# A bf16 copy for the transposes of quantised activations, in a fused two-layer AdaLN/FFN kernel

## What is computed

```python
def _fake_quant_lastdim(x):
    s = jnp.max(jnp.abs(x), axis=-1, keepdims=True) / QMAX      # QMAX = 127
    s = jnp.maximum(s, 1e-08)
    return jnp.clip(jnp.round(x / s), -QMAX, QMAX) * s

def _dyn_quant_linear(x, w, b):
    return jnp.einsum('bti,oi->bto', _fake_quant_lastdim(x), _fake_quant_lastdim(w)) + b

h = jnp.einsum('bij,bkj->bik', x, weight[adapter_ids])          # "l0"
h = _layernorm(h, gamma, beta)
h = _dyn_quant_linear(h, w1, b1)
h = jax.nn.gelu(h, approximate=False)
h = _dyn_quant_linear(h, w3, b3)
x = x + h
```

## Time and profile before

| | us |
|---|---|
| median of 3 runs | 876.65 |
| lowest, highest | 874.74, 877.16 |
| the profiled execution, its own time | 874.75 |
| its span, first to last instruction | 872.8 |

### The profile page before, as it was taken

The page is one execution under the profiler, slowest core; times in us unless marked ns, Lnnn a source line. Parts: engine busy times, 40 slices in busy tenths (PEclk is TensorE's granted clock), DMA queues, the critical chain, the costliest instruction groups (busy, mean ns, idle before and its releaser), DMA issues.

```text
span 872.8 us, 11055 instructions
## 1 busy us (share of the span) xinstructions
PE 761.2 (87%) x3172; PEld 488.5 (56%) x3172; DVE 578.2 (66%) x2036; ACT 335.4 (38%) x577; POOL 64.7 (7%) x34
## 2 busy tenths in 40 slices
PE   4989899989899999998968899999898892699656
PEld 2544444344444444444645788887687771587445
DVE  6555282434675656483746524438999998899998
ACT  0333733304534252434324633444333421757152
POOL 0002000202621011022020000000000000000000
PEclk9999999989999999999999899999999996899969
DMA  8994654133448353512031345334333249653103
GB/s 340 374 334 163 240 179 171 60 111 140 159 149 355 108 189 139 193 56 89 24 121 50 129 161 182 115 114 159 122 128 108 102 155 411 272 193 121 48 35 158
DMA packets 40297, 140.94 MB, mean 161 GB/s; under 512 B 8511, under 2 KB 9663, under 8 KB 34626
## 3 DMA queue, kind: packets, MB, share of 16 engines
q1 hardware_dynamic: 38962, 137.72, 43.8%
q10 hardware_dynamic: 1296, 2.74, 0.8%
HBM read 106.86 MB, written 33.58 MB: 161 GB/s over the span
## 4 chain that ended last, share of the span: by engine, by line
PE 49%; DVE 34%; ACT 8%; issue 5%; DMA 2%; POOL 1%; DVEq 0%; SPq 0%; ACTq 0%
PE PS L779 21%; PE PS L837 12%; PE PS L947 8%; DVE ksum L1361 6%; DVE kprod L1356 6%; DVE ka L1365 4%; DVE nr L1438 4%; DVE kb L1365 3%; PE PS L826 2%; ACT qT L542 2%; DVE xr L1283 2%; PE PS L868 2%; DMA x_raw<-x_tr_dram 2%; PE PS L794 1%; DVE xp L1268 1%
## 5 line engine op out<-in xcount | busy, mean ns | idle before, releaser
L779 PE MATMUL PS<-w_raw,x_raw 128*128 128x512 f32 x512 | 230.4, 604 | 13.7 <-DMA x_raw<-x_tr_dram 11.0
L779 PEld LDWEIGHTS PS<-w_raw,x_raw 128*128 128x128 f32 x512 | 96.7, 194 | 124.9 <-issue 124.1
L947 PE MATMUL PS<-w_hi,xT_hi 128*128 128x512 f32 x256 | 105.0, 410 | 0.0
L947 PE MATMUL PS<-w_lo,xT_hi 128*128 128x512 f32 x256 | 102.0, 399 | 0.0
L947 PE MATMUL PS<-w_hi,xT_lo 128*128 128x512 f32 x256 | 101.7, 397 | 0.0
L1361 DVE TENSOR_REDUCE ksum<-kprod 128x16 f32<-128x64 f32 x392 | 75.2, 233 | 0.2 <-issue 0.2
L837 PE MATMUL PS<-w3q,qT 128*128 128x512 bf16 x256 | 61.3, 395 | 14.4 <-ACT qT L542 14.4
L1131 DVE SCALAR_TENSOR_TENSOR gbuf<-PS,lnst,vecs 128x512 f32<-128x512 f32 x32 | 23.7, 749 | 75.0 <-PE PS L837 75.0
L542 ACT ACTIVATE qT<-PS,round_c 128x512 bf16<-128x512 f32 x64 | 40.3, 679 | 84.4 <-PE PS L826 84.3
L837 PE MATMUL PS<-w1q,qT 128*128 128x512 bf16 x256 | 60.4, 391 | 8.4 <-DVE x1buf L1149 5.7
L470 POOL TENSOR_TENSOR xres<-xres,vecs 128x1024 f32<-128x1024 f32 x16 | 42.2, 2659 | 329.8 <-DMA xres<-x_tok_dram 329.8
(11 more groups left out here) (165 smaller groups left out, 1128.2 us busy)
## 6 DMA issues: line engine op xcount, KB each, us to landing
w_raw<-cond_w_dram SPq DMA_DIRECT2D x32, 1024.0 KB, 5.6
stage<-w_dram SPq DMA_DIRECT2D x16, 512.0 KB, 12.1
x_raw<-x_tr_dram SPq DMA_DIRECT2D x32, 256.0 KB, 6.4
xres<-x_tok_dram SPq DMA_DIRECT2D x8, 1024.0 KB, 9.3
x_scratch<-x1buf SPq DMA_DIRECT2D x16, 512.0 KB, 6.4
x1n<-x_scratch SPq DMA_DIRECT2D x16, 512.0 KB, 5.7
xr<-x_scratch SPq DMA_DIRECT2D x16, 512.0 KB, 3.6
y_scratch<-y SPq DMA_DIRECT2D x16, 512.0 KB, 3.6
```

Of the source, the lines that this page charges most:

```text
L779: mm = pe.matmul(PS[:, 2 * t + h, :], x_raw[pr][:, c, t * P:(t + 1) * P], w_raw[pr][:, c, h * H2:(h + 1) * H2], start=(pr == 0 and c == 0) ...
L947: pe.matmul(PS[:, 2 * t + h, :], xx[:, c, t * P:(t + 1) * P], ws[c // 2][:, c % 2, h * H2:(h + 1) * H2], start=(c == 0 and xx is xT_hi and ...
```

## The change

ScalarE gets a second ACTIVATE behind each quantising one: it reads the f32 tile, subtracts `ROUND` and writes a bf16 copy `q16[t]`. It waits on a semaphore (`r1_done`, `r2_done`) for the first. The integers from -127 to 127 are exact in bf16. TensorE transposes `q16[t]` with a bf16 identity, all eight blocks into one bank (8 x 128 bf16 columns fill its 2 KB): tile 0 uses `T_BANK`, tile 1 `T_BANK + 1`. `evac_T` becomes one ACTIVATE of 128x1024, a plain copy, which waits for all eight. To make room, `av_hi` and `av_lo` shrink to the 56 columns in use (`AW`), and what reads them follows. VectorE makes the bf16 identity at the start.

```diff
+    AW = 32 + NH
...
+        ident16 = sb("ident16", [P, P], BF16)
+        av_hi = sb("av_hi", [P, KC, AW], F32R)
+        av_lo = sb("av_lo", [P, KC, AW], F32R)
...
+        q16 = [sa(f"q16{t}", [P, D], BF16) for t in range(NTOK)]
...
             def quant1(s, t):
                 act.wait_ge(ln_step, LN_OPS * (NTOK * s + t + 1))
                 nc.scalar.activation(hbuf[t][:, :], hbuf[t][:, :], ACT.Identity, bias=round_c[:, 0:1],
-                                     scale=lnst[:, t, 9:10]).then_inc(q1_done, 1)
+                                     scale=lnst[:, t, 9:10]).then_inc(r1_done, 1)
+                act.wait_ge(r1_done, NTOK * s + t + 1)
+                nc.scalar.activation(q16[t][:, :], hbuf[t][:, :], ACT.Identity, bias=round_c[:, 1:2]).then_inc(q1_done, 1)
...
             def evac_T(s, t, which):
...
-                for h in range(2):
-                    act.wait_ge(done, 4 * s + 2 * t + h + 1)
-                    nc.scalar.activation(qT[t][:, 4 * h:4 * h + 4, :],
-                                         PS[:, T_BANK + h, :].rearrange("p (c n) -> p c n", c=4),
-                                         ACT.Identity, bias=round_c[:, 1:2]).then_inc(ev, 1)
+                act.wait_ge(done, 4 * s + 2 * t + 2)
+                nc.scalar.activation(qT[t][:, :, :], PS[:, T_BANK + t, :].bitcast(BF16).rearrange("p (c n) -> p c n", c=KC),
+                                     ACT.Copy).then_inc(ev, 2)
...
             def transposes(s, t, which):
-                q, done, src = (q1_done, t1_done, hbuf) if which == 1 else (q2_done, t3_done, gbuf)
+                q, done = (q1_done, t1_done) if which == 1 else (q2_done, t3_done)
                 pe.wait_ge(q, NTOK * s + t + 1)
+                t_bank_free(s, t, which)
+                bank = PS[:, T_BANK + t, :].bitcast(BF16)
                 for h in range(2):
-                    t_bank_free(s, t, which, h)
-                    for c in range(4):
-                        tr = pe.transpose(PS[:, T_BANK + h, c * P:(c + 1) * P],
-                                          src[t][:, (4 * h + c) * P:(4 * h + c + 1) * P], ident[:, :])
+                    for c in range(4 * h, 4 * h + 4):
+                        tr = pe.transpose(bank[:, c * P:(c + 1) * P], q16[t][:, c * P:(c + 1) * P], ident16[:, :])
                     tr.then_inc(done, 1)
...
-                        mm = pe.matmul(PS[:, LL_BANK, 0:S], a[:, c, :], xx[:, c, :],
+                        mm = pe.matmul(PS[0:AW, LL_BANK, 0:S], a[:, c, :], xx[:, c, :],
...
+            dve.wait_ge(id_set, 1)
+            nc.vector.tensor_copy(ident16[:, :], ident[:, :]).then_inc(id16_set, 1)
```

More of the change, by code:

```diff
@@ L88, in adaln_ffn @@
         ident = sb("ident", [P, P], F32)
-        av_hi = sb("av_hi", [P, KC, P], F32R)
-        av_lo = sb("av_lo", [P, KC, P], F32R)
+        ident16 = sb("ident16", [P, P], BF16)
+        av_hi = sb("av_hi", [P, KC, AW], F32R)
+        av_lo = sb("av_lo", [P, KC, AW], F32R)
         zall = sb("zall", [P, NT, NH], F32)
@@ L162, in adaln_ffn @@
         vec_ld, bias_ld, ids_ld, ones_set = sem("vec_ld"), sem("bias_ld"), sem("ids_ld"), sem("ones_set")
-        id_zero, id_set = sem("id_zero"), sem("id_set")
+        id_zero, id_set, id16_set = sem("id_zero"), sem("id_set"), sem("id16_set")
+        r1_done, r2_done = sem("r1_done"), sem("r2_done")
         misc_ld, wb_split, b_set, b_ld = sem("misc_ld"), sem("wb_split"), sem("b_set"), sem("b_ld")
@@ L530, in quant2 @@
                 nc.scalar.activation(gbuf[t][:, :], gbuf[t][:, :], ACT.Identity, bias=round_c[:, 0:1],
-                                     scale=q2st[:, t, 2:3]).then_inc(q2_done, 1)
+                                     scale=q2st[:, t, 2:3]).then_inc(r2_done, 1)
+                act.wait_ge(r2_done, NTOK * s + t + 1)
+                nc.scalar.activation(q16[t][:, :], gbuf[t][:, :], ACT.Identity, bias=round_c[:, 1:2]).then_inc(q2_done, 1)
             def evac_T(s, t, which):
@@ L652, in evac_ll @@
                 act.wait_ge(ll_done, b + 1)
-                nc.scalar.activation(fbuf[:, :], PS[:, LL_BANK, 0:S], ACT.Copy)
+                nc.scalar.activation(fbuf[0:AW, :], PS[0:AW, LL_BANK, 0:S], ACT.Copy)
                 nc.scalar.activation(ls[0:RANK, :], PS[0:RANK, LL_BANK, 0:S], ACT.Copy)
@@ L769, in _ @@
             pe.wait_ge(id_set, 1)
+            pe.wait_ge(id16_set, 1)
             def l0(s, pr):
@@ L796, in stage_T, with t_bank_free @@
                     tr.then_inc(st_T, 1)
-            def t_bank_free(s, t, which, h):
+            def t_bank_free(s, t, which):
                 if which == 1 and s == 0:
-                    pe.wait_ge(st_ev, 2 * (KC + 3 + 2 * t) + h + 1)
-                elif which == 3 and s == 0 and t == 0:
-                    pe.wait_ge(st_ev, 2 * (KC + 7) + h + 1)
-                elif which == 3 and s == NB - 2 and t == 0:
-                    pe.wait_ge(xl_done, 2 + h + 1)
-                elif t == 1:
-                    pe.wait_ge(e1_done if which == 1 else e3_done, 4 * s + h + 1)
+                    pe.wait_ge(st_ev, 2 * (KC + 3 + 2 * t) + 2)
+                elif which == 3 and s == 0:
+                    pe.wait_ge(st_ev, 2 * (KC + 7) + 2)
+                elif which == 3 and s == NB - 2:
+                    pe.wait_ge(xl_done, 4)
                 elif which == 1:
-                    wait(pe, e3_done, 4 * (s - 1) + 2 + h + 1)
+                    pe.wait_ge(e3_done, 4 * (s - 1) + 2 * t + 2)
                 else:
-                    pe.wait_ge(e1_done, 4 * s + 2 + h + 1)
+                    pe.wait_ge(e1_done, 4 * s + 2 * t + 2)
             def o_bank_free(s, t, which, h):
@@ L960, in heads @@
                 for t in range(NTOK):
-                    pe.matmul(PS[:, LG_BANK, t * NH:(t + 1) * NH], fbuf[:, t * P:(t + 1) * P], ident[:, VC:VC + NH],
+                    pe.matmul(PS[:, LG_BANK, t * NH:(t + 1) * NH], fbuf[0:AW, t * P:(t + 1) * P], ident[0:AW, VC:VC + NH],
                               start=True, stop=False)
```

## The result

The changed kernel takes 889.09 us, median of 4 runs (887.36 to 889.62), against 875.69 for the kernel before (4 runs, 872.34 to 877.16): a ratio of 1.0155, 95% interval 1.0121 to 1.0189. It is slower by 13.4 us. The forecast was 7.5 us and 884.2, in a range of 876.5 to 890. So the direction, the mechanism and the range held, and the size was off by 5 to 6 us. The profiled execution has 889.62 us as its own time and a span of 887.5.

What follows compares the result with a forecast made beforehand. TensorE is nearly full, but ScalarE's queue ends each step on a TensorE stall. Path changes of +0.8 us plus clock falls of +6.7 make +7.5, added to the 876.65 median: 884.2, range 876.5 to 890.

Steps and rivals of the forecast that it cites:

- The walk: Running sum of delays from start to tail, clock aside: +0.8 us at the end of the span.
- the start's 0.74 + 1.16: Start: first transposes wait for both evacuations, +0.74; a copy delays later evacuations, 1.16; given as +1.8 at `l0(2,0)`.
- rival 3: Transposes don't get shorter, the weight load setting the pace: +10.3 us, 887; chance 0.07.
- the stall chain: `quant2`, copy and evacuation ahead of `product(s-1,0,3)` at a step's end: net +0.91 us where on the path.
- the places at the edge: `product(s-1,0,3)` in steps 4, 5, 6 and `product(6,0,3)`: idles of 2.36 or some 2.3 us; half counted, 3.4.
- the larger ones: Start's last weight block, `l0(4,3)`, `product(7,0,3)`: idles of 2.99, 2.7, 3.1 us; three quarters counted, 3.3.
- the seven: All places where a lengthened stall might drop TensorE's clock, four at the edge and three larger: 11.1 us if all fall.
- its own sign: Forecast wrong if a step's chain no longer passes through the copy, or idles of 2.4 leave the clock at 1.00.
- the av weights: 24 narrower matmuls in `low_and_heads` of 0 and 1: 0.25 us off twice, bounds 0 and -0.6.
- the clock holds: Rival: clock stays up in all or all but one place, 877.5 to 879.1; chance 0.15.
- the kernel is faster: Rival: copy cheap or hidden in ScalarE's queue between `quant2` and `evac_T`; -2.6, or -9.6 if off the path; chance 0.08.
- It falls everywhere: Rival: the clock falls at every listed place, 888.6 us; chance 0.10.

Runs made afterwards that it cites:

- experiment 12: Kernel before, with tile 0's second evacuation ahead of tile 1's gelu (steps 3 to 6) and step 4's x_raw requested right behind the base weights; 868.02 us.
- experiment 4: Kernel before with only the av weights narrowed from 128 to 56 columns; 877.04 us, ratio 1.0017.
- Experiment 3: Changed kernel with eight extra bf16 matmuls filling TensorE's stall in each of steps 4 to 7; 887.78 us, ratio 1.0131.
- experiment 1: Kernel before plus the copies, which nobody reads, and the narrow av weights; transposes stay f32; 890.2 us, ratio 1.0183.
- experiment 5: Changed kernel with the heads' products contracting over all 128 rows again; 887.52 us, ratio 1.0145.
- experiments 2 and 7: Changed kernel without copies: in 2 quantising writes bf16 without rounding, 873.43 us; in 7 it writes fp16 with 1536 added, 873.52 us.
- experiment 6: Changed kernel with all 32 copies, some moved back in ScalarE's queue, and tile 0's second evacuation moved ahead in steps 3 to 6; 878.09 us.
- experiment 9: Changed kernel with fp16 quantising instead of copies, heads over 128 rows, and tile 0's second evacuation moved ahead in steps 3 to 6; 873.6 us.

## Why the prediction was right, and where its sizes were off

Marks of TensorE in the two profiled executions, the changed kernel's start minus the one before. The first 65 us, where nothing on TensorE was changed, are already 2.5 us apart (65.11 and 67.61): the first load came 0.3 later, and the first products ran at the low clock for longer (9.9 and 9.9 for 8.8 and 8.8). Kernels whose start is the same differ there as much, from 8.6 and 8.8 in experiment 12 to 9.7 and 9.8 in experiment 4, so it belongs to the run. It is taken off below.

| mark | forecast without clock | measured | of that, clock | the rest |
|---|---|---|---|---|
| `l0(2,0)` starts | +1.8 | +2.9 | 1.1 | +1.8 |
| `l0(3,0)` | +0.1 | +2.5 | 2.3 | +0.2 |
| `product(1,1,3)`, step 3 | -0.1 | +0.6 | 0.6 | 0.0 |
| `product(3,0,3)`, behind step 4's end | +1.9 | +4.6 | 1.3 | +3.3 |
| `product(5,0,3)` | +1.1 | +5.9 | 3.0 | +2.9 |
| `product(7,0,3)` | in the tail | +9.7 | 6.0 | +3.7 |
| end of the span | +0.8 | +12.2 | 7.6 | +4.6 |

The walk holds to 0.1 us up to step 3, is 1.4 short behind step 4, loses 0.4 more in steps 5 and 6, and parts again behind them. Two slips in the prediction's sums change nothing: the start's 0.74 + 1.16 is 1.9 and not 1.8, and rival 3's 14 x 0.43 is 6.0 and not 6.2.

The clock column sums how much longer single products took than at the full clock, after less before: the start up to `l0(2,0)` 1.1, `l0(2,0)` 1.2, `l0(3,1)` -1.7 (a fall that the kernel before had and this one not), `product(2,0,3)` 0.7, `product(4,0,3)` and `product(5,0,3)` 1.7 each, `product(7,0,1)` 1.3, `product(7,0,3)` 1.6. The 1.1 of the start is what reached `l0(2,0)`: of the 1.5 lost at `product(0,1,1)` the last weight block saw 0.7, and the group of transposes ahead of `l0(2,0)` took 0.4 longer. Experiment 3, with the same start and the clock held at `product(0,1,1)`, stands at +1.8 there, less its own 2.0 at the first products.

**Right: the path.** The copy in ScalarE's queue between `quant2` and `evac_T` lengthens each step (the step of 47.17 in experiment 1, the stall chain in the trace). Product to product was 45.81 where the clock held (45.58 from 288.09 to 333.67, and the missing 0.23) and 47.50 where it fell (333.67 to 381.17), forecast 45.6 and 47.3. The idle before `product(s-1,0,3)` was 2.35 (near 2.4), that before `l0(4,3)` 2.39 (near 2.7).

**Right: the prices.** The copy 1.15 (1.14), the evacuation 1.01 (1.02), the transposes 0.45 a group (0.45). The Trainium skill's 81 ns for a load and a matmul of 128 columns ("TensorE: Matmul & The Clock Gate", section Back-to-back issue gap), weighed in the prediction, does not hold for this stream: 0.45 / 8 is 56 ns. One small thing went the other way: an `l0` behind a bf16 group takes 6.92 on the chain, not 6.87, and the eight of steps 5 and 6 make the 0.4 lost there.

**Right in the sum, not in the places: the clock.** Forecast 6.7, measured 7.6. The prediction counted a half of the places at the edge and three quarters of the larger ones; of the seven, `l0(4,3)`, `product(3,0,3)` and `product(6,0,3)` held. By its own sign ("if idles of 2.4 leave the clock at 1.00") the rule that idles of this size fall failed in one of the three middle steps. Falls came at `product(0,1,1)` and, deeper than before, at `product(2,0,3)` and `product(7,0,1)`, which were not on the list, and one of before went away. That the two numbers are close is partly luck.

**Wrong: the av weights.** The step put them at -0.5, with bounds of 0 and -0.6. They gained 0.12 and 0.06 in the two groups on the chain and cost 0.52 a batch in the heads, on the chain three times. Experiment 4 puts the part at +1.6 and experiment 5 puts the heads at +1.6; three batches are 1.56. The error was not in a number but in what was looked at: the diff says "what reads them follows", and I priced the 24 matmuls and not their reader. Against the -0.5 that is some 2.1 us of the 5.9 by which the forecast fell short (13.4 against 7.5).

**Left out: VectorE's wait at the end of step 3.** Forecast without clock +2.0 from `product(1,1,3)` to `product(3,0,3)` (-0.1 to +1.9), measured 3.3 (4.0 less 0.7 of clock). The copy on the way to `split_hi(3)` (1.15) and the longer stall (0.91) are there. What is not in the sum is VectorE's addition ahead of them, in the chain that ends step 3; it is 1.3 of the 1.9 us by which the stall before `product(2,0,3)` grew (4.26, has 2.37). VectorE and GpSimd in the kernel before, then in the changed one:

```profile
223.30 2.56 DVE L1135 TENSOR_TENSOR gbuf<-gbuf,vecs 128x1024 f32<-128x1024 f32 x1
...
220.24 4.53 POOL L464 TENSOR_TENSOR w_lo<-w_raw,w_hi 128x2048 fp32r<-128x2048 f32 x1 [11.97 <-ACT w_hi L498]
```

```profile
225.51 3.87 DVE L1142 TENSOR_TENSOR gbuf<-gbuf,vecs 128x1024 f32<-128x1024 f32 x1
...
223.79 4.51 POOL L468 TENSOR_TENSOR w_lo<-w_raw,w_hi 128x2048 fp32r<-128x2048 f32 x1 [12.35 <-ACT w_hi L502]
```

Alone this addition takes 1.24 us. In both kernels it ends 1.1 us after GpSimd's split (225.86 and 224.77; 229.38 and 228.30), whenever it began. But for some 0.15 us at its start, it stood still as long as GpSimd ran. The copy behind `quant2(2,0)`, which stands ahead of `split_hi(1)`, made GpSimd start later, so that the two overlap by 2.8 us and no longer by 1.5: 1.3 us more on the path. In experiments 2 and 7, without copies, and in 6, which puts this copy behind `split_hi(1)`, the addition takes 2.7 us; in 3 and 5, with it, 3.9. The Trainium skill ("SBUF — State Buffer", section SBUF: two separate sides) calls the port pair that the two engines share an exclusive lock held for a whole instruction, against which a VectorE instruction with two SBUF inputs waits; this trace agrees, with 1.1 us from the end of the one to the end of the other in both kernels.

So of the 5.9 us, some 2.1 are the av weights and their reader, 1.4 the steps 3 and 4, 0.4 the `l0`s of steps 5 and 6, and 0.9 the clock. Another 1.0 is the late start of that one execution (2.5) less what the two profiled executions lie further apart than their medians (1.5), and no cause in the kernel is shown for it.

**The rivals.** That the clock holds (877.5 to 879.1), that the transposes don't get shorter (0.87 a group) and that the kernel is faster are out. "It falls everywhere", 888.6, came nearest in time, for another reason than its own: three of the seven places held. The rival by which the copies are hidden was about the queue, and experiment 6 shows what was right in it: against experiment 9, and its heads' 1.6, the 32 copies cost some 3 us once they stand elsewhere in it.

## What to carry to other kernels

An instruction added to an engine that is busy 38% of the time costs its full length wherever it stands between a value and the engine that waits for it; read the queue of that engine from the last producer to the consumer, and look first whether something in it can go behind. What a faster engine gains is worth nothing ahead of a wait that another chain sets: here the load before `l0(4,3)` swallowed the gain of three different edits, until the transfer itself was asked for earlier. When a diff narrows an operand "to make room", price every instruction that reads the result too.
